# Rows moved for the experts by sorting them into pieces of three on TensorE, and one indirect scatter for each column

## What is computed

```python
h = tok(x, W, b, pos_embed)                      # (16, 1024, 64)
h = h + attn(layernorm(h))                       # softmax over tokens for K, over heads' columns for Q
z = layernorm(h)
probs = softmax(z @ gate_w + gate_b)             # 16 experts
top_probs, top_idx = top_k(probs, 2)             # two experts for a token, weights made to sum to 1
hidden = silu(z @ w1[e]) * (z @ w2[e])           # 64 -> 128, for each chosen expert e
h = h + sum over the two chosen e of weight[e] * (hidden @ w3[e])
```

## Time and profile before

| | |
|---|---|
| time, median of 3 runs | 790.79 us (790.71 to 795.49) |
| span of the profiled execution | 791.9 us |
| busy: PE / DVE / ACT / POOL | 578.2 / 441.7 / 347.6 / 518.2 us |
| indirect DMAs of POOL | 256 scatters (L497), 256 gathers (L514) |
| mean granted TensorE clock | 0.873 |
| DMA, mean | 118 GB/s |

### The profile page before, as it was taken

The page is one execution under the profiler, slowest core; times in us unless marked ns, Lnnn a source line. Parts: engine busy times, 40 slices in busy tenths (PEclk is TensorE's granted clock), DMA queues, the critical chain, the costliest instruction groups (busy, mean ns, idle before and its releaser), DMA issues.

```text
span 791.9 us, 14201 instructions
## 1 busy us (share of the span) xinstructions
PE 578.2 (73%) x3856; PEld 476.0 (60%) x3856; DVE 441.7 (56%) x1237; ACT 347.6 (44%) x753; POOL 518.2 (65%) x540
## 2 busy tenths in 40 slices
PE   5967796787799989998899889998958702883000
PEld 3455545574588678867786678687958702873000
DVE  5664755556447686676667567756765601454111
ACT  2124122152456476647564566446626701674111
POOL 2052246576771777777777777777777777777774
PEclk9976796798999999999999999979979965996555
DMA  2499022333553375528542744374345414544111
GB/s 78 101 229 396 28 71 83 97 97 90 148 170 89 72 188 142 144 53 208 136 124 69 190 130 121 76 175 109 112 117 128 114 51 127 135 100 98 40 40 31
DMA packets 168871, 93.20 MB, mean 118 GB/s; under 512 B 99680, under 2 KB 152928, under 8 KB 168800
## 3 DMA queue, kind: packets, MB, share of 16 engines
q1 hardware_dynamic: 151632, 66.71, 32.1%
q0 software_dynamic: 16384, 25.20, 11.6%
q10 hardware_dynamic: 784, 0.39, 0.2%
HBM read 45.06 MB, written 47.19 MB: 116 GB/s over the span
## 4 chain that ended last, share of the span: by engine, by line
POOL 33%; PE 29%; issue 15%; DVE 13%; DMA 7%; ACT 3%; POOLq 0%; ACTq 0%; DVEq 0%; SPq 0%
POOL rows_scratch L497 15%; POOL sums L514 14%; PE wide_ps L1030 5%; PE h_ps L1169 4%; PE y_ps L1186 3%; DMA hx<-xi_scratch 3%; DMA xi_scratch<-xi 2%; POOL hx L514 2%; POOL kexp L514 2%; PE turn_ps L1153 2%; PE wide_ps L1050 2%; PE wide_ps L1129 1%; PE hidT_ps L1179 1%; PE wide_ps L1036 1%; DVE twice_y L970 1%
## 5 line engine op out<-in xcount | busy, mean ns | idle before, releaser
L497 POOL DMA_INDIRECT rows_scratch<-z_parts,place x256 | 254.9, 996 | 128.4 <-issue 74.7
L514 POOL DMA_INDIRECT sums<-y_scratch,place x224 | 213.8, 955 | 82.7 <-issue 66.4
L1169 PE MATMUL h_ps<-w_hi,rowsT 128*128 x384 | 111.5, 320 | 40.9 <-DVE hid_all L972 33.8
L970 DVE SCALAR_TENSOR_TENSOR twice_y<-tanh,h_ps 128x256 f32<-128x256 f32 x192 | 79.8, 416 | 101.3 <-ACT tanh L618 85.3
L1169 PEld LDWEIGHTS h_ps<-w_hi,rowsT 128*128 128x128 f32 x384 | 74.6, 194 | 55.8 <-issue 54.5
L1186 PE MATMUL y_ps<-w_sb,hidT_all 128*128 x768 | 100.9, 276 | 1.1 <-ACT twice_y L631 1.1
L1169 PE MATMUL h_ps<-w_lo,rowsT 128*128 x384 | 101.0, 290 | 0.0
L1186 PEld LDWEIGHTS y_ps<-w_sb,hidT_all 128*128 128x128 f32 x768 | 97.4, 199 | 2.2 <-issue 2.2
L1153 PE MATMUL turn_ps<-ident,rows_all 128*128 128x128 f32 x384 | 60.8, 282 | 46.3 <-DMA rows_all<-rows_scratch 39.8
L618 ACT ACTIVATE tanh<-h_ps 128x256 f32<-128x256 f32 x192 | 69.8, 387 | 56.3 <-PE h_ps L1169 50.0
L972 DVE SCALAR_TENSOR_TENSOR hid_all<-twice_y,h_ps 128x256 f32<-128x256 f32 x192 | 80.8, 421 | 6.6
(11 more groups left out here) (252 smaller groups left out, 910.3 us busy)
## 6 DMA issues: line engine op xcount, KB each, us to landing
rows_all<-rows_scratch SPq DMA_DIRECT2D x96, 256.0 KB
y_scratch<-twice_y SPq DMA_DIRECT2D x96, 128.0 KB
rows_scratch<-tanh SPq DMA_DIRECT2D x3, 3072.0 KB, 19.4
xi_scratch<-xi SPq DMA_DIRECT2D x16, 256.0 KB
rows_scratch<-z_parts,place POOLq DMA_INDIRECT x256
hx<-xi_scratch SPq DMA_DIRECT2D x14, 256.0 KB
sums<-y_scratch,place POOLq DMA_INDIRECT x224
out<-sums SPq DMA_DIRECT2D x56, 64.0 KB
```

The lines of the kernel that those rows point to most:

```text
L497: gp.indirect_dma_start(rows_dram[n], bass.IndirectOffsetOnAxis(ap=place[m % RING][:, r, j:j + 1], axis=0), z_parts[m % 2][:, j // 2, j % ...
L514: gp.indirect_dma_start(y_of[r][apart(m)][:, j // 2, j % 2, :], None, y_dram[m % 3], bass.IndirectOffsetOnAxis(ap=place[m % RING][:, r, j: ...
L970: ve.scalar_tensor_tensor(twice[:, j, :], tanh[:, j, :], 1.0, halves[:, j, 0, :], ALU.add, ALU.mult).then_inc(S["twice_done"], 1)
L1169: mm = te.matmul(h_ps[:, j * 256:(j + 1) * 256], rowsT[g % 2][:, j * P:(j + 1) * P], w[:, bass.ds(experts[g][j], 1), :, :].rearrange("d a ...
```

## The change

1. **Pieces.** A column's 256 rows (128 tokens, two experts each) are sorted by expert into pieces of `PIECE` = 3 rows of one expert. At most (256 + 16 x 2) / 3 = 96 pieces are needed (`PIECES`); unused places in a piece stay zero.
2. **The sort.** For each column DVE builds a matrix `route` (128 tokens x 3 x 96, ones and zeros) with two instructions (`find_routes`), PE multiplies it by `z_parts` in three matmuls, one for each place in a piece (`move_rows`), into one PSUM bank, and ACT copies the 96 x 384 result to `pieces` (`take_piece`). Three route buffers and four piece buffers are there, one PSUM bank (two for pair 0).
3. **The scatter.** GpSimd issues one indirect DMA of 96 pieces of 1536 bytes for each column instead of two of 128 rows of 512 bytes: 128 in all for 256. The gathers stay as they are, in other steps.
4. **Tiles.** A tile is 42 pieces, 126 rows (`R`) instead of 128. As pieces are not always full, a pair needs `GROUPS` = 13 groups, 104 in all. Transposes, copies, loads and stores of the groups work on 126 rows.
5. **Counting.** Places are worked out in pieces, over columns and experts, from constant matrices that GpSimd builds at the start (`sort_consts`, 29 instructions ahead of `split_experts`). The 15 small matmuls of L1137 go; two rounds between PE and DVE (counts, then tiles) take the place of one, and pair 2's counting moves from step k = 14 to k = 17.
6. **Banks.** The bank `hidT_ps` is given to the pieces (`piece_ps`). turn_hidden now writes `turn_ps`, the bank that turn uses too, so each of the two waits until ACT has copied the other's result. In PE's step project_out now stands before turn.
7. **Steps.** The columns of pairs 3 to 7 are sorted one in each half step from step 13m + 7 on. The last project_in (g = 103) is in step 126.

```diff
+ROUTES = (29, 42, 64) + tuple(2 * (13 * m + 7) for m in range(3, PAIRS))
+GATHER = tuple(LAG + 13 * m + 16 for m in range(PAIRS))
+GATHER_STEPS = 9
+SUMS = [[GATHER[m] + (4 + 2 * q if m < PAIRS - 1 else 1 + q) for q in range(4)] for m in range(PAIRS)]
...
-                for r in range(2):
-                    gp.indirect_dma_start(rows_dram[n], bass.IndirectOffsetOnAxis(ap=place[m % RING][:, r, j:j + 1], axis=0),
-                                          z_parts[m % 2][:, j // 2, j % 2, :, :].rearrange("p n e -> p (n e)").bitcast(F32),
-                                          None).then_inc(scattered[n], 16)
+                wait(pool, "piece_ready", COLS * m + j + 1)
+                gp.indirect_dma_start(pieces_dram[n], bass.IndirectOffsetOnAxis(ap=piece_at[m % 2][0:PIECES, j:j + 1], axis=0),
+                                      pieces[j % PIECE_RING][0:PIECES, :], None).then_inc(scattered[j % PIECE_RING], 16)
...
+            def take_piece(m, j):
+                n = j % PIECE_RING
+                wait(act, "piece_ps_ready", COLS * m + j + 1)
+                wait_on(act, scattered[n], 16 * (COLS // PIECE_RING * m + j // PIECE_RING))
+                sc.activation(pieces[n][0:PIECES, :], piece_place(m, j)[0:PIECES, 0:PIECE * 2 * E], ACT.Copy).then_inc(S["piece_ready"], 1)
...
+            def find_routes(m, js):
+
+                for j in js:
+                    i = COLS * m + j
+                    wait(dve, "slot_ready", m + 1)
+                    wait(dve, "piece_ps_ready", i - ROUTE_RING + 1)
+                    ve.tensor_scalar(route[i % ROUTE_RING][:, :, :], slot_id[:, :, :], slot[:, 0, j:j + 1], None,
+                                     ALU.is_equal).then_inc(S["route_begun"], 1)
+                for j in js:
+                    i = COLS * m + j
+                    wait(dve, "route_begun", i + 1)
+                    ve.scalar_tensor_tensor(route[i % ROUTE_RING][:, :, :], slot_id[:, :, :], slot[:, 1, j:j + 1],
+                                            route[i % ROUTE_RING][:, :, :].bitcast(F32), ALU.is_equal, ALU.add).then_inc(S["route_ready"], 1)
...
                     multiply(g)
+                for m, js in routes_of(2 * s):
+                    find_routes(m, js)
                 for m, k in steps_at(s):
                     attend(m, k + 0.5)
+                for m, js in routes_of(2 * s + 1):
+                    find_routes(m, js)
...
+            def move_rows(m, j):
+
+                i = COLS * m + j
...
+                wait(pe, "route_ready", i + 1)
+                wait(pe, "piece_ready", i - 1 if m == 0 else i)
+                for n in range(PIECE):
+                    mm = te.matmul(piece_place(m, j)[0:PIECES, n * 2 * E:(n + 1) * 2 * E], route[i % ROUTE_RING][:, n, :],
+                                   z_parts[m % 2][:, j // 2, j % 2, :, :].rearrange("p n e -> p (n e)"), start=True, stop=True)
+                mm.then_inc(S["piece_ps_ready"], 1)
```

370 lines of the change are left out of this document (271 added, 99 removed).

## The result

The changed kernel takes 948.67 us (median, 945.35 to 955.2) where the kernel before takes 792.48 beside it: 1.196 times as long, 95% interval 1.190 to 1.202. The prediction had the direction, 813 us with a range of 779 to 844, and missed the size by 136 us. The profiled execution lasts 947.6 us (before: 791.9).

What follows compares the result with a forecast made beforehand. POOL was taken to bound from 290 us on, PE to set the pace elsewhere. 791.9 - 39.8 - 18.3 + 28.7 - 10 + 40 + 22 = 814.5, so 813 us as median; range 779 to 844.

Steps and rivals of the forecast that it cites:

- Waits for rows, -39.8: PE's two waits for rows scattered late: both go, as a pair's scatters and gathers need less POOL time; -39.8 us.
- The tail, -18.3: Behind the last store: pair 6's gathers are done by then, only pair 7's remain, 48.2 us instead of 66.5; -18.3 us.
- Price of a scatter: POOL's indirect DMAs: about 1.27 us each with issue, 48 left in a pair, 61 us.
- "Moved at no cost", the shared bank: Turn's wait for the copy of `hidT`: covered by 0.1 us before project_out's issue ends, so nothing added.
- My rival for the bank: Turn stalls where ACT is late with `hidT` because attention's copies wait for DVE: +37, 850 us; chance 0.03.
- "Eight more groups, +28.7": Eight added groups after the attention at 3.59 us each; +28.7 us.
- "Counting, -10": Counting on PE: fewer small matmuls, -6, and the `hot_sum` waits gone less a second PE-DVE round, -4; -10 us.
- "The sort on PE, +40": PE's three matmuls for each of 112 columns at 0.12 us; +40 us, bounds 27 and 74.
- "Waits for the route, +22": PE's next group waits for DVE's route at the step's end: 3 us for each of pairs 1 to 6, 0.5 in eight steps; +22.
- ACT's copies, "covered": ACT's 128 piece copies, about 0.5 us each, come after the copy of `hidT`: nothing; uncovered, 64 us at worst.
- Pair 0's columns, "counted at nothing; were they not, +6": Pair 0's sort on PE, in slices where PE is busy 6 to 7 of 10: nothing, otherwise +6 us.
- "Steps without attention still 3.6 us": Sign that the forecast is right: steps without attention keep 3.6 us, 29 of them at the end.

Runs made afterwards that it cites:

- e3: The kernel before with project_out ahead of turn and, on top, hidden values and rows turned in one shared PSUM bank, without the sort; 815.6 us (1.028).
- e2: The kernel before with one change: project_out of group g-2 stands ahead of the turn of group g+2's rows; 793.4 us (0.9999).
- e4: The changed kernel without the sort itself (no routes, moves or piece copies; scatters write constant data); 843.6 us (1.057).
- e11: The changed kernel with four matmuls that nothing reads ahead of TensorE's wait for the keys' exponentials, in five pairs; 919.4 us (1.155).
- e7: The changed kernel without ScalarE's piece copies alone; the scatters write constant data once their column's moves are done; 903.1 us (1.135).
- e6: The changed kernel without TensorE's moves alone (three matmuls a column); routes and piece copies stay; 872.6 us (1.100).

## Why the prediction was wrong, step by step

*Waits for rows, -39.8:* right, the wait is gone. *The tail, -18.3:* right; the last store is issued at 896.27 us and 51.3 us lie behind it, where I had 48.2 and 2.3 for its landing; -17.3 counted from the last `project_in`. *Price of a scatter:* right. The waits for rows and the tail are what the change was worth, 57 us, and they were paid.

*"Moved at no cost", the shared bank:* the step that failed first. I compared the end of the copy with the end of `project_out`'s issue and stopped there; what stands behind the turn in PE's order is the register load. 22 us of time (e3 less e2) and 46 us of TensorE's in the groups, against nothing. A step without attention went from 3.6 to 4.3 us; in steps with attention the bank brings a second wait, that of `turn_hidden` for the copy of the rows (33.6 us in e3), at which my sum did not look. My rival for the bank had 37 us and copies that come late for attention, right in kind though at the other of the two waits, and a chance of only 0.03.

*"Eight more groups, +28.7":* the mechanism held, the price did not: 4.25 us for 3.59, so 34.

*"Counting, -10":* the sign was wrong. I counted PE's matmuls and left out DVE's `find_ends`, 4.3 us long ahead of the keys' maximum: k = 6 goes from 6.2 to 9.7 us between e3 and e4, k = 7 from 4.8 to 6.0. Over the four pairs in which the two meet, k = 6 and 7 take 43.9 us in e3 and 64.7 in e4: 21 us the other way, half clock included.

*"The sort on PE, +40" and "Waits for the route, +22":* 105 us (949 less e4's 844) against 62. The matmul was overpriced if anything (0.087 for 0.12), and PE's direct waits for the route are 15.6 us, near the 22 of the sum. What failed is the chain behind the route. I had 0.1 us for the signal, 0.36 for the matmuls and 0.6 for the register load, 1.06 in all, and the load was mis-sized: it begins 0.06 us after the route and the next group 1.73 us after it at the earliest, 1.8 in all, and what holds it is not the route alone but the piece copy too. From 88.1 to 104.2 us a period grows by 16.1. Some 17 us more of it are at half clock, at 0.47 worth 8 us, so half of the growth is the clock; the other half is work and the bare register load (k = 10: 4.3 to 5.7, k = 12: 4.6 to 5.6, both at full clock). That split is an estimate from e11's price. ACT's copies, "covered", give 46 us when they go (e7): a move waits for the copy of the piece ahead of it.

*Pair 0's columns, "counted at nothing; were they not, +6":* the groups begin 16.4 us later. 7.6 of it are there without the sort (e4 begins at 165.5 against e3's 157.9; as this start varies by 5 us between kernels that are the same up to there, that is a rough number). The other 10 are the moves: without them (e6) the groups begin at 164.9.

*Missing in the sum altogether:* the clock. Every duration came from rows at full clock; 33 us of each period of the changed kernel run at half of it.

The bill, from the profiled executions, 791.9 to 947.6 us: GpSimd freed -57, the shared bank +46, eight groups +34, `find_ends` in k = 6 and 7 +21, a later start without the sort +6, the sort +103. That leaves 2 us open. The step from e3 to e4 (812.2 to 844.2) is the test of it, for it holds neither the bank nor the sort: the later start +7.6, the stand for rows -25.7, the tail -9.4, eight groups +34, k = 6 and 7 +20.8, and 4.7 us that I can't place.

What the prediction said would show itself did: POOL idle between scatters, no wait for `rows_all`, PE waiting for `route`, periods over 80. "Steps without attention still 3.6 us" is the one that came out clearly wrong (4.3), and the one that would have told of the bank. That the direction came out right is in part luck: the sum lay only 2.8% above the kernel before, and the terms that it had at nothing or with the wrong sign, the bank, `find_ends` and the clock, all pointed the same way.

## What to carry to other kernels

When a wait is added to an in-order engine, price what is queued behind the waiting instruction, register loads above all, not only the instruction itself: here the wait cost its own matmuls nothing and a step without attention 0.65 us. And take the length of such a load from its own rows, not from the idle time that is left bare. When TensorE gets more waits, price everything behind them at the lower clock too; matmuls that nothing reads, put where it would stand idle, can pay for themselves (-29 us in e11, -7 us on the kernel before). And if single parts of a change, taken out one by one, give more than the whole, look for a loss that each of them removes, here the half clock in two steps.
